# The negated row maxima of an attention kernel placed by two one-row transfers instead of one two-row transfer

## The reference

```python
x = x + jnp.tanh(g_xattn[0]) * xattn(_layernorm(x), ctx, ctx, ...)
x = x + jnp.tanh(g_ffn[0]) * ffn(_layernorm(x), ...)
# in xattn, for 16 heads, 4 parts m of each, dk = 16:
qh, kh, vh = (interfere(proj(q)), interfere(proj(k)), interfere(proj(v)))
scores = jnp.einsum('bhqdm,bhkdm->bhqkm', qh, kh) / math.sqrt(dk)
weights = jax.nn.softmax(scores, axis=3)
out = jnp.einsum('bhqkm,bhkdm->bhqdm', weights, vh)
```

## Time and profile before

| | us |
|---|---|
| median of three runs | 1385.08 |
| the profiled execution's own time | 1385.08 |
| its span | 1383.3 |
| TensorE (PE) busy | 1356.9 (98%) |
| VectorE (DVE) busy | 671.6 (49%) |
| GpSimd (POOL) busy | 400.8 (29%) |
| ScalarE (ACT) busy | 399.4 (29%) |

### The profile page before, as it was taken

How to read it: one execution, slowest core, us unless ns; L and a number is a source line. 1 busy time by engine, 2 the same in 40 slices (tenths; PEclk the granted TensorE clock), 3 DMA queues, 4 the chain that set the end, 5 groups by cost and what they waited for, 6 DMA issues and landing times.

```text
span 1383.3 us, 22229 instructions
## 1 busy us (share of the span) xinstructions
PE 1356.9 (98%) x8464; PEld 1129.5 (82%) x8464; DVE 671.6 (49%) x1356; ACT 399.4 (29%) x727; POOL 400.8 (29%) x599
## 2 busy tenths in 40 slices
PE   7999999999999999989999999999999999999998
PEld 7888888888878888778888888888778878878787
DVE  5323122121485444566777777777965144253110
ACT  3321010111222222255555555555451020111100
POOL 1069991000130000245656565565600000000000
PEclk9999999999999999999999999999999999999999
DMA  5774553644646776798888887777442202211011
GB/s 205 211 214 152 141 154 133 143 153 128 168 168 150 185 178 165 219 280 251 239 230 236 230 230 220 219 221 222 181 175 107 76 16 91 77 61 61 31 42 50
DMA packets 187065, 221.86 MB, mean 160 GB/s; under 512 B 26320, under 2 KB 124752, under 8 KB 186960
## 3 DMA queue, kind: packets, MB, share of 16 engines
q1 hardware_dynamic: 161040, 182.17, 45.6%
q10 hardware_dynamic: 25920, 38.28, 9.5%
HBM read 135.45 MB, written 83.89 MB: 159 GB/s over the span
## 4 chain that ended last, share of the span: by engine, by line
PE 92%; DMA 2%; DVE 2%; issue 1%; ACT 1%; ACTq 1%; POOL 1%; SPq 0%; POOLq 0%
PE bank L160 20%; PE bank L162 20%; PE bank L161 20%; PE bank L1391 5%; PE bank L1411 4%; PE bank L1372 4%; PE bank L1374 4%; PE bank L1373 4%; PE bank L1426 4%; PE bank L309 2%; PE bank L346 2%; PE bank L1398 1%; ACTq L514 1%; DMA q_in<-neg 1%; DMA wo_raw<-in_wo_rows 1%
## 5 line engine op out<-in xcount | busy, mean ns | idle before, releaser
L1577 DVE TRANSPOSE_TENSOR_REDUCE part<-bank 128x16 f32<-128x512 f32 x256 | 174.3, 692 | 2.8 <-PE bank L1391 0.3
L1523 ACT ACTIVATE probT<-bank 128x512 f32<-128x512 f32 x256 | 138.9, 595 | 92.3 <-PE bank L1411 88.8
L160 PE MATMUL bank<-place_a,w_hi 128*128 128x512 f32 x384 | 152.5, 397 | 1.8 <-DVE place_a L153 1.8
L162 PE MATMUL bank<-place_a,w_lo 128*128 128x512 f32 x384 | 150.6, 392 | 0.0
L161 PE MATMUL bank<-place_a,w_hi 128*128 128x512 f32 x384 | 149.4, 389 | 0.0
L548 DVE SCALAR_TENSOR_TENSOR stage_lo<-bank,bias_mixed,stage_hi 128x512 fp32r<-128x512 f32 x46 | 34.6, 751 | 175.5 <-ACT stage_hi L550 175.5
L1372 PE MATMUL bank<-w_hi,oT_hi 128*128 128x512 f32 x256 | 109.0, 426 | 2.2 <-POOL oT_lo L1697 1.7
L1202 DVE SCALAR_TENSOR_TENSOR raw_d<-bank,gates,raw_d 128x512 f32<-128x512 f32 x32 | 24.0, 750 | 170.4 <-PE bank L162 170.4
L160 PE MATMUL bank<-place_b,place_a 128*128 128x512 f32 x256 | 102.1, 399 | 0.0
L161 PE MATMUL bank<-place_c,place_a 128*128 128x512 f32 x256 | 102.0, 398 | 0.0
L160 PE MATMUL bank<-w_hi,yT_hi 128*128 128x512 f32 x256 | 101.7, 397 | 0.0
(11 more groups left out here) (233 smaller groups left out, 2835.1 us busy)
## 6 DMA issues: line engine op xcount, KB each, us to landing
k_rows<-stage_hi SPq DMA_DIRECT2D x128, 128.0 KB, 2.5
v_pad<-v_out SPq DMA_DIRECT2D x32, 512.0 KB, 2.6
v_place<-v_pad ACTq DMA_DIRECT2D x64, 256.0 KB, 4.3
k_in<-k_rows SPq DMA_DIRECT2D x64, 192.0 KB, 3.2
q_in<-q_rows SPq DMA_DIRECT2D x128, 96.0 KB, 3.4
q_rows<-wq_own SPq DMA_DIRECT2D x78, 128.0 KB, 2.5
raw_d<-x_mid SPq DMA_DIRECT2D x17, 512.0 KB, 3.4
early_q<-q_rows SPq DMA_DIRECT2D x90, 96.0 KB, 3.5
```

The source lines that it names most:

```text
L160: nc.tensor.matmul(bank_ap, sh, mh, start=(i == 0), stop=False)
L162: last = nc.tensor.matmul(bank_ap, sl, mh, start=False, stop=(i == len(chunks) - 1))
L1523: act.activation(probT[o % NPT][:, i].rearrange("k a p q -> k (a p q)"), two_bank[i][:], ACT.Exp).then_inc(s_exp, 1)
L1577: dve.tensor_reduce(part[o % NS][:, :, 2 * i:2 * i + 2, :].rearrange("k a p b -> k a (p b)"), one_bank[i][:].rearrange("k (a b t) -> k a b ...
```

## The change

`place_max` issues two transfers where it issued one. The first copies the high part (partitions 0 to 31 of `neg`) into row `ROWS` of `q_in` once `s_nhi` has come; the second copies the low part (partitions 32 to 63) into row `ROWS + 1` once `s_nlo` has come. Each adds 16 to `s_neg`, so the two places that wait for it (TensorE ahead of the second pass, GpSimd ahead of the reuse of a `neg` buffer six octets later) wait for 32 an octet. The bytes copied are the same.

```diff
                 def place_max(o):
-                    sp.wait_ge(s_nlo, o + 1)
-                    sp.dma_start(q_in[o % KQ][ROWS:ALL].rearrange("r a p (b t) -> r (a p b) t", t=32).bitcast(F32),
-                                  neg[o % NS][:].bitcast(F32)).then_inc(s_neg[o % KQ], 16)
+                    for i, ready in enumerate((s_nhi, s_nlo)):
+                        sp.wait_ge(ready, o + 1)
+                        sp.dma_start(
+                            q_in[o % KQ][ROWS + i:ROWS + i + 1].rearrange("r a p (b t) -> r (a p b) t", t=32).bitcast(F32),
+                            neg[o % NS][32 * i:32 * i + 32].bitcast(F32)).then_inc(s_neg[o % KQ], 16)
@@ second_pass
-                        pe.wait_ge(s_neg[slot], 16 * (o // KQ + 1))
+                        pe.wait_ge(s_neg[slot], 32 * (o // KQ + 1))
@@ gpsimd
-                            pool.wait_ge(s_neg[(s - NS) % KQ], 16 * ((s - NS) // KQ + 1))
+                            pool.wait_ge(s_neg[(s - NS) % KQ], 32 * ((s - NS) // KQ + 1))
```

## The result

The changed kernel took 1398.04 us (median of 4 runs, 1393.66 to 1399.24) against 1385.39 us of the kernel before on the same chip. The ratio is 1.0084, 95% interval [1.0055, 1.0113]. It is slower by about 12 us, beyond the range of the prediction; the forecast was 1382.6 us. Nine more runs of the changed kernel on record, the profiled one among them, lie between 1390.61 and 1401.01 us, all above the slowest of the four before (1386.76). The profiled execution took 1395.75 us, with a span of 1393.9 us.

What follows compares the result with a forecast made beforehand. TensorE was taken to bound the steady stretch, with the DMA engines full in the opening. Maxima waits -2.1, `oT_lo` -0.8 and a remaining wait +0.4 gave -2.5 us, from 1385.08 to 1382.6 us; range 1378.3 to 1388.3 us.

Steps and rivals of the forecast that it cites:

- the hold of an issue: On SyncE's queue, each new transfer was to hold it 0.43 us, making 0.37 us extra an octet.
- upper bound of 0.57: On SyncE's queue, the most extra time an octet, in us, if each new transfer held it like the old one.
- In the steady stretch this is hidden.: From 640 to 950 us, SyncE's extra fits in its 0.86 us of waiting an octet; cost 0.
- The fourth rival: Whole attention phase: SyncE becomes the bound from a hold of 0.68 us, 1502 us at the longest hold; chance 0.03.
- 2.2 us of earlier landing: In the opening, spreading over 16 DMA engines instead of 2 lands the maxima 1.9 to 2.6 us sooner, called 2.2.
- forecast credit of 2.1 + 0.8 us: In the opening, TensorE's waits for the maxima (2.1 us) and for `oT_lo` (0.8 us) were to go.
- the wait for `oT_lo`: In the opening, TensorE's 0.8 us wait, traced to a weight chunk's load issued at 619.49, was counted as gone.
- the slower rival: In the opening, SyncE's queue is full and six transfers run up to 3.4 us late: 1388.5 or 1391.9 us; chance 0.16.
- second low stretch: In the opening, gaps might bring TensorE another stretch at low clock, 3.4 us more, giving 1391.9 us.
- that on the number of engines: A copy gets the largest number up to 16 dividing both sides' slowest dimension, size 1 aside: 2 engines before, 16 after.

Runs made afterwards that it cites:

- e11: Kernel before plus one extra SyncE issue an octet ahead of the old transfer, its 32 rows of 96 bytes written to 32 partitions; 1389.4 us, ratio 1.0034.
- e6: Changed kernel's two transfers from octet 16 on only, the old single transfer in octets 0 to 15; 1389.59 us, ratio 1.0039 to the kernel before.
- e1: Kernel before plus one extra SyncE issue an octet (32 rows of 96 bytes to an unread tile) ahead of the old transfer; 1390.56 us, ratio 1.0038.
- e2: Against the kernel before, one transfer of 32 rows places only the high part of the maxima, the low row staying zero; 1386.86 us, ratio 1.0007.
- e3: Changed kernel with the low part's transfer issued from ScalarE's queue instead of SyncE's; 1385.92 us, ratio 1.0014 to the kernel before.
- e4: Kernel before with its old two-row transfer issued from ScalarE's queue instead of SyncE's; 1388.38 us, ratio 1.0022.
- e8: Changed kernel with both transfers of maxima behind the slot's loads of keys and queries instead of ahead; 1399.14 us, ratio 1.0107 to the kernel before.
- e7: Changed kernel plus one extra SyncE issue an octet (32 rows of 96 bytes to an unread tile) ahead of its two; 1485.51 us, ratio 1.0737.

## Why the prediction was wrong

The first step that failed is a term: the hold of an issue. The prediction took 0.43 us, with 0.53, the old transfer's own, as the bound from above. The two measured 0.51 and 0.59, and the load of keys behind them held 0.15 us more. The prediction took its value from transfers of another kind, the loads from HBM, and never asked whether an issue changes the next one's hold. The extra of an octet was 0.76 us by the medians, 0.79 by the totals, instead of 0.37, above the upper bound of 0.57.

The second follows from it: "In the steady stretch this is hidden. [...] The term is 0." The comparison was the right one, extra against waiting. The number it had to stay under was 0.86 us by the waits, 0.77 by the pauses and 0.73 by what is free in them, and 0.79 is over it. That the average wait exceeds the extra isn't enough, either: before the change the two query loads of an octet held SyncE 1.47 and 1.50 us in two of every eight octets and 0.89 to 1.24 in the others, so the queue gets late in some octets, and only left-over pauses make that up. That this unevenness is why e11 still lost something with some 7 us left is my reading; no run changes it alone. Without any pause (e6, 1.6 us) the steady stretch pays 6 us; with some 7 us (e1) it pays 1. The fourth rival named this mechanism, with 0.68 us as the hold from which it decides, and got 0.03. With the mean hold of the new transfers, 0.604 us, and the keys' extra of 0.15 spread over the two, 0.68 us is what it came to (0.604 + 0.15/2 = 0.68). I had priced that rival at its far end alone (117 us), and not at its threshold, where it turned out to lie.

The third: the spread over 16 engines happened, but "2.2 us of earlier landing" in the opening brought nothing. The landings from 602 to 611 did shorten, for the earlier trace rows:

```profile
k_in<-k_rows SPq DMA_DIRECT2D x2, 192.0 KB, 3.9
q_in<-q_rows SPq DMA_DIRECT2D x4, 96.0 KB, 4.3
...
q_in<-neg SPq DMA_DIRECT2D x2, 4.0 KB, 4.4
```

but there SyncE issued less in the same time (DMA share 0.90 for 1.03), so this isn't evidence of the spread. e2, with the spread and a normal queue, waited 4.4 us for the maxima in the opening and gained nothing in time. The forecast credit of 2.1 + 0.8 us wasn't there; the wait for `oT_lo`, counted as gone, was 1.5 us in the changed kernel.

The mechanism of the slower rival, "SyncE's queue is full in the opening", was right: in octets 5 to 15 the maxima were issued on average 4.5 us after their low part was ready (0.9 us before the change), and 6.6 us were lost. The rival had priced 3.4 us, or 6.8 with a second low stretch, so its upper price fits in size. Its second stretch didn't come: TensorE's low clock stayed one stretch, but longer; from the kernel after:

```profile
615.00:632.00 17.00, 12.46 (x107) 9.68 (x105) 9.97 (x21) 8.13 (x15) 6.41 (x13) 0.70 0.87 242
```

17 x 0.30 = 5.1 us of clock instead of the 3.4 of the earlier trace rows. That is 1.7 us more; together with the 4.7 us of idle time that TensorE gained from 584 to 636 it comes near the 6.6.

Of the Trainium skill's two rules in the prediction, that on the number of engines ("DMA: Bandwidth & Descriptors", section "Why a DMA increments its semaphore by 16 and not by 1") holds for the new shape as well: 96 packets. The same page's "Rules for kernel authors" advise against two transfers to disjoint halves, because the halves share the same engines, and that advice was the better guide. I set it aside because the old transfer used 2 engines and not 16. It held for another reason than the page's, the issue's cost on SyncE's queue: in e3 both halves still run on the engines, and the steady stretch takes what it took before.

## What to carry to other kernels

Count a queue's time like an engine's: the holds of all its issues per round of the loop against the round's length. What is left is the budget for another issue, and it must stay well above zero, not just positive. Use mean holds and not medians for it, and leave out the gap that passes ahead of any issue. Take the hold of a new transfer from the most similar one in kind (here small rows between tiles in SBUF), not in number of rows, and allow something for its neighbour. Halving a transfer to start its first half sooner pays only if the consumer can use a half.

## What the runs showed of the hardware that I had not expected

- The hold of an issue on SyncE depends on what came before it. The load of keys held 0.304 us behind a pause (e4), 0.426 right behind the old two-row transfer, 0.578 right behind a transfer of 32 rows of 128 bytes, and 0.31 behind the same transfer with a pause between (11 times in e8). The old transfer held 0.53 us behind a query load and 0.57 to 0.58 behind the extra issue; neither the number of rows of that one (31 or 32) nor the form of its destination explained it. The cause is open.
- A transfer of 64 small rows on 2 DMA engines held SyncE 0.527 us, one of 32 rows on 16 engines 0.51 behind a load, with a pause between (e2) or without (the changed kernel), one of 31 rows 0.617. What came before isn't all: the same extra transfer of 32 rows of 96 bytes, behind a query load each time, held 0.553 us in e1, where the two-row transfer followed it, and 0.509 in e7, where a one-row one did.
- The kernels, whose projections are the same, reached the attention phase at 576 or at 580 us in different profiles, under either form of the change (576.2, 576.4, 575.9, 575.7, 575.8; 580.1, 580.4, 580.0, 580.2). Where in the projections this arises isn't known.
